# Gate logits of a top-2 mixture of experts from split fp32r operands in one column group, where four column groups multiplied fp32

## The reference

```python
x = L0_attn_data                                   # (4, 512, 1024)
block_mask = mask.reshape(32, 32, 32, 32).sum(axis=(1, 3)) > 0
w_masked = weight * repeat(block_mask)             # (1024, 1024)
x = x + einsum('bsk,nk->bsn', layernorm(x), w_masked)

z = layernorm(x)
logits = z @ W_gate + b_gate                       # 8 experts
_, top_idx = top_k(logits, 2)
y_all = relu(einsum('bsd,edh->bseh', z, W_e) + b_e)
x = x + take_along_axis(y_all, top_idx).mean(over the two)
```

## Time and profile before

| | us |
|---|---|
| median of 3 runs | 709.16 |
| lowest and highest run | 708.97, 710.17 |
| profiled execution | 709.16 |
| its span in the trace | 707.4 |
| TensorE busy | 681.8 |
| VectorE busy | 325.2 |
| ScalarE busy | 240.1 |
| GpSimd busy | 286.6 |

### The profile page before, as it was taken

How to read it: one execution, slowest core, us unless ns; L and a number is a source line. 1 busy time by engine, 2 the same in 40 slices (tenths; PEclk the granted TensorE clock), 3 DMA queues, 4 the chain that set the end, 5 groups by cost and what they waited for, 6 DMA issues and landing times.

```text
span 707.4 us, 11264 instructions
## 1 busy us (share of the span) xinstructions
PE 681.8 (96%) x3617; PEld 559.9 (79%) x3617; DVE 325.2 (46%) x667; ACT 240.1 (34%) x323; POOL 286.6 (41%) x254
## 2 busy tenths in 40 slices
PE   5999999999899999999999999999999999999993
PEld 5667888877678888888888888888888888888883
DVE  4669787888998653343341540351542530000000
ACT  4832212212421434434343434343434343434330
POOL 6421212115445245454445454445454544444330
PEclk9799999999999999999999999999999999999998
DMA  8725445467754459687686683686594855232323
GB/s 318 307 89 176 184 149 209 133 251 249 243 197 150 149 156 245 165 224 202 149 261 151 167 233 82 149 264 150 169 246 101 230 145 115 37 57 34 57 34 56
DMA packets 34501, 118.21 MB, mean 167 GB/s; under 512 B 5776, under 2 KB 5776, under 8 KB 34448
## 3 DMA queue, kind: packets, MB, share of 16 engines
q1 hardware_dynamic: 22032, 80.23, 31.7%
q0 software_dynamic: 11232, 37.23, 25.8%
q10 hardware_dynamic: 1184, 0.04, 0.1%
HBM read 83.40 MB, written 37.75 MB: 171 GB/s over the span
## 4 chain that ended last, share of the span: by engine, by line
PE 85%; DVE 7%; issue 3%; DMA 2%; POOL 1%; SPq 1%; ACT 1%; POOLq 0%; DVEq 0%
PE psO L335 77%; PE psT L437 5%; DMA mask_stage<-L_attn_mask 2%; PE psT L358 1%; DVE st L691 1%; PE psG L470 1%; DVE xr L718 1%; DVE st L699 1%; POOL rs L1035 0%; DVE x2T L718 0%; ACT wT L566 0%; PE psT L376 0%; SPq L273 0%; SPq L274 0%; POOLq L46 0%
## 5 line engine op out<-in xcount | busy, mean ns | idle before, releaser
L335 PE MATMUL psO<-slots,xT 128*128 (+1 forms) x1872 | 435.9, 392 | 0.0
L335 PEld LDWEIGHTS psO<-slots,xT 128*128 128x128 f32 x1872 | 348.2, 188 | 70.7
L335 PE MATMUL psO<-wT,xT 128*128 128x512 f32 x768 | 182.8, 394 | 0.2 <-ACT wT L566 0.2
L335 PEld LDWEIGHTS psO<-wT,xT 128*128 128x128 f32 x768 | 141.7, 188 | 28.6 <-ACT wT L566 0.3
L1081 POOL DMA_INDIRECT rows_out<-xb,tok_of x37 | 63.8, 1725 | 220.9 <-ACT xb L659 214.5
L845 DVE CAST slots<-raw 128x1024 fp32r<-128x1024 f32 x56 | 53.6, 957 | 193.7 <-PE psO L335 105.3
L659 ACT ACTIVATE xb<-psO 128x512 f32<-128x512 f32 x78 | 46.8, 600 | 252.8 <-PE psO L335 252.8
L1075 POOL TENSOR_TENSOR xT<-x2T,xT 128x1024 fp32r<-128x1024 f32 x38 | 100.3, 2640 | 17.7 <-ACT x2T L638 17.4
L847 DVE TENSOR_TENSOR slots<-raw,slots 128x1024 fp32r<-128x1024 f32 x56 | 75.1, 1342 | 1.9
L600 ACT ACTIVATE psO<-bias_slot 128x512 f32 (+1 forms) x78 | 47.1, 604 | 36.7 <-ACT xb L659 17.0
L1020 POOL TENSOR_SCALAR rs<-mv 128x1 f32<-128x1 f32 x16 | 4.5, 280 | 109.1 <-DVE mv L693 109.1
(11 more groups left out here) (162 smaller groups left out, 425.5 us busy)
## 6 DMA issues: line engine op xcount, KB each, us to landing
raw<-L_ffn_W_e SPq DMA_DIRECT2D x56, 512.0 KB, 5.2
xb<-data_t SPq DMA_DIRECT2D x16, 512.0 KB, 4.2
x_rows<-x SPq DMA_DIRECT2D x16, 512.0 KB, 5.1
xr<-L_attn_data SPq DMA_DIRECT2D x11, 512.0 KB, 6.0
rows_out<-xr SPq DMA_DIRECT2D x11, 512.0 KB, 2.7
mask_stage<-L_attn_mask SPq DMA_DIRECT2D x8, 512.0 KB, 11.2
w_stage<-L_attn_weight SPq DMA_DIRECT2D x8, 512.0 KB, 11.8
bias_slot<-L_ffn_b_e SPq DMA_DIRECT2D x8, 512.0 KB, 6.0
```

The costliest lines, as they stand in the source:

```text
L335: last = eng.matmul(psum, xT[:, p, a, kt, :], moving(b, kt), start=(i == 0 and kt == 0 and not seeded), stop=(i == len(PASSES) - 1 and kt ...
```

## The change

The gate product is made from the split operands. `gates` becomes fp32r, with 32 columns for each group of features: HI and LO of each of its two old parts. The 16 matmuls of a block multiply it with `xT`, first its HI and then its LO part, and all accumulate in partitions 0 to 31 of `psG`, that is in one column group. `gated` and `fold` have 32 rows, and L455 adds up the four combinations of HI and LO instead of the four quarters. VectorE makes the LO parts of `gates` once, with two subtractions behind the copies, and the memset of the 16 empty columns goes. As the gate no longer reads `xb`, `load_x` no longer waits for `c_gate`, and it is called for block i + 3 in place of i + 2.

```diff
-        gates = sb("gates", [P, KT, 32], F32)
-        fold = sb("fold", [P, 2 * N_EXP], F32)
-        gated = sb("gated", [P, P], F32)
+        gates = sb("gates", [P, KT, 2, 2, N_EXP], F32R)
+        fold = sb("fold", [4 * N_EXP, 2 * N_EXP], F32)
+        gated = sb("gated", [4 * N_EXP, P], F32)
...
                 if t >= 2:
                     eng.wait_ge(c_xlo, t - 1)
-                    eng.wait_ge(c_gate, t - 1)
...
-                if 2 <= i + 2 < NB:
-                    load_x(i + 2)
+                if 2 <= i + 3 < NB:
+                    load_x(i + 3)
...
-                        eng.wait_ge(c_gw, GATES)
+                        eng.wait_ge(c_gw, 5)
...
-                    for kt in range(KT):
-                        q = kt % N_QUART
-                        last = eng.matmul(psG[32 * q:32 * q + 32, 0:P], gates[:, kt, :], xb[:, i % 2, kt * P:(kt + 1) * P],
-                                          start=(kt < N_QUART), stop=(kt >= KT - N_QUART))
+                    for part in (HI, LO):
+                        for kt in range(KT):
+                            last = eng.matmul(psG[0:4 * N_EXP, 0:P], gates[:, kt, :, :, :].rearrange("p a b e -> p (a b e)"),
+                                              xT[:, i % 2, part, kt, :], start=(part == HI and kt == 0),
+                                              stop=(part == LO and kt == KT - 1))
...
-                    eng.activation(gated[:], psG[:, 0:P], ACT.Copy).then_inc(c_gated, 1)
+                    eng.activation(gated[:], psG[0:4 * N_EXP, 0:P], ACT.Copy).then_inc(c_gated, 1)
...
-            quarters = ident[:].rearrange("p (q x) -> p x q", q=N_QUART)
-            eng.tensor_reduce(fold[:], quarters[:, 0:2 * N_EXP, :], AX.X, ALU.add).then_inc(c_prep, 1)
-            eng.memset(gates[:, :, 2 * N_EXP:], 0.0).then_inc(c_gw, 1)
+            eng.tensor_tensor(fold[:], ident[0:4 * N_EXP, 0:2 * N_EXP], ident[0:4 * N_EXP, 2 * N_EXP:4 * N_EXP], ALU.add).then_inc(c_prep, 1)
...
-            eng.tensor_copy(gates[:, :, 0:N_EXP], wg[:]).then_inc(c_gw, 1)
-            eng.tensor_copy(gates[:, :, N_EXP:2 * N_EXP].rearrange("p (q c) e -> p q c e", q=N_QUART), folded).then_inc(c_gw, 1)
+            of_folded = lambda part: gates[:, :, part, 1, :].rearrange("p (q c) e -> p q c e", q=N_QUART)
+            eng.tensor_copy(gates[:, :, HI, 0, :], wg[:]).then_inc(c_gw, 1)
+            eng.tensor_copy(of_folded(HI), folded).then_inc(c_gw, 1)
             eng.tensor_copy(wg_sum[:], psW).then_inc(c_gw, 1)
+            eng.wait_ge(c_gw, 2)
+            eng.tensor_tensor(gates[:, :, LO, 0, :], wg[:], gates[:, :, HI, 0, :].bitcast(F32), ALU.subtract).then_inc(c_gw, 1)
+            eng.tensor_tensor(of_folded(LO), folded, of_folded(HI).bitcast(F32), ALU.subtract).then_inc(c_gw, 1)
```

More of the change, by code:

```diff
@@ L236, in build @@
         c_first, c_pick = sem("c_first"), sem("c_pick")
-        ST, TOP, HOT, RS1, RS2, GATES = 3, 12, 8, 2, 4, 4
+        ST, TOP, HOT, RS1, RS2 = 3, 12, 8, 2, 4
         FIRST_KNOWN, FIRST_TOK = 4, 15
```

## The result

The changed kernel takes 714.55 us (median of 6 runs, 714.40 to 714.75), the kernel before, on the same chip, 709.07 (6 runs, 708.20 to 710.17). The ratio is 1.0078, with a 95% interval of 1.0065 to 1.0091: slower by 5.5 us. The forecast of 717.3 was right in sign and 2.8 us too high.

A forecast was written before the change was run, and what follows sets the result against it. TensorE was taken to bound most rounds, VectorE six. Gate +0.53 and fold +0.29 us over 16 blocks make 13.1; less 4.8 hidden and 0.2 at the start, +8.1 on 709.2 gives 717.3 us, range 712.8 to 730.

The forecast's parts named there:

- The bound and the place: Token-block loop, 46.6 to 236 us: time added to TensorE is kernel time, except where TensorE waits anyway.
- The step of the narrow fp32r matmul: Gate matmuls in one column group: 0.063 us from start to start, 0.95 from first to last.
- (a): Gate: the next weight load doesn't hide, step 0.083 us, gate +0.83 a block, 722 us; chance 0.12.
- (b): Gate: a narrow fp32r matmul takes 0.11 us like fp32, gate +1.28 a block, 729.5 us; chance 0.10.
- (c): Gate: a narrow fp32r matmul takes 0.229 us like a wide one, gate +3.17 a block, 760 us; chance 0.12.
- The gate's price: Gate matmuls L470 on TensorE: +0.53 us a block, 0.43 to 0.61 by the two readings.
- Rival (d): Gate: matmuls of one column group overlap, step below 0.027 us, drain and fold save up to 0.2 a block, 707; chance 0.03.
- The fold: Fold matmul L455 in a 32-row tile: draining and unhidden weight loads add 0.29 us a block, between 0 and 0.35.
- the case without the fold's cost: Fold matmul's smaller tile needs no drain: ten blocks pay 0.53 us each, 714 us; chance 0.13.
- Six rounds hidden: Six VectorE-bound rounds of the loop hide 4.8 us of their 4.9 us added TensorE time.
- The rest at nothing: VectorE's two subtractions, the dropped memset, ACT's smaller copy and the earlier loads of x: no gain or cost.
- The sum: Whole kernel: 13.1 us for 16 blocks, less 4.8 hidden and 0.2 at the first fold, gives +8.1 us.

The follow-up runs named there:

- the run in one column group: The kernel before with its eight fp32 gate matmuls all in column group 0: 723.80 us, ratio 1.0212.
- the run with 128 rows: The changed kernel, but `gated` and `fold` keep 128 rows, 96 of them zero: 711.58 us, ratio 1.0048.
- the runs in fp32r: The changed kernel with `gated` and `fold` in fp32r instead of fp32: 712.90 us with 32 rows, 710.24 us with 128 rows.
- the changed kernel with spread slices: The changed kernel with the first expert's weight chunks split over rounds 10 to 15 as 1, 1, 2, 1, 2, 1: 713.44 us, ratio 1.0073.

## Why the prediction was right, and where it was off

**The bound and the place: right.** Time added to TensorE in the loop is time of the kernel; nothing changed after 236 us.

**The step of the narrow fp32r matmul: right.** Forecast 0.063 us and 0.95 from first to last; measured 0.0605 and 0.91 (1.13 - 0.22). Rivals (a), (b) and (c), with 0.083, 0.11 and 0.229, are out; the loads of 32 columns add nothing that shows. The 0.11 of a fp32 matmul, which the prediction read from two L420 that are transposes in the code, was borne out by the run in one column group (1.66/15). The Trainium skill's 81 ns a matmul ("TensorE: Matmul & The Clock Gate", "Back-to-back issue gap"), with which the 722 us of (a) agreed, is too high for this stream.

**The gate's price: mis-sized.** This is the term that was off. "First to last start is then 15 x 0.063 = 0.95, against 0.37" counts only what lies inside the group, plus 0.05 for a shorter last stream. But the old group had 0.10 + 0.21 us at its two seams and the new one has 0.03 + 0.06, which is 0.22 saved and not 0.05. So the gate costs 0.54 - 0.22 = +0.32 a block and not +0.53, which lies below the stated 0.43 to 0.61. One seam stood in the rows: the earlier trace rows puts the first L470 0.10 behind the last L376 (65.70 against 65.41 + 0.36 - 0.17 = 65.60), four times the step of that group. Rival (d) did name the drain that would be saved, but as part of a case with a chance of 0.03. The same drain stood in the fold's term, which took it from L391, a fp32 matmul in a narrow tile, and was not carried over to the gate, where it was about to go.

**The fold: right.** Forecast +0.29 a block and 0.66 against 0.37 in the step; measured 0.64 against 0.37, and 0.31 a round with the late start of the projection behind it. The time alone would not have told: 714.55 is nearer to the 714 of the case without the fold's cost. The step of 0.64 and the run with 128 rows show that it was paid, while the gate cost less. The analogy from a change of columns to one of rows held in size; the runs in fp32r show that it is not one thing, since only that of the rows is paid in both types. The Trainium skill, "TensorEngine Tiling (Array Packing)", Key Properties, says that changing the tiling mode drains TensorE. The fold's rows agree (0.26 to 0.27 us in either type), the fp32 gate's too (0.3 for both sides); the fp32r gate's matmuls, in the same 128x32 tile between full ones, show no drain.

**Six rounds hidden: right.** 3.8 us of waits gone, with 0.64 a round, where 0.82 a round was to take all 4.8; doubling the gate in these rounds cost nothing and in others its full price.

**The rest at nothing: right** within half a microsecond, by the run with the loads undone for the loads; the first gate matmul, at 45.5 to 45.8 in the kernels with the new preparation and no long low-clock stretch, is 0.1 to 0.2 later than in those with the old one. VectorE's spare time has grown. Its wait for the projection in one early round, before and after:

```profile
72.09 0.75 DVE L718 SCALAR_TENSOR_TENSOR xr<-psO,kept,xr 128x512 f32<-128x512 f32 x1 [0.38 <-PE psO L335]
72.79 0.75 DVE L718 SCALAR_TENSOR_TENSOR xr<-psO,kept,xr 128x512 f32<-128x512 f32 x1 [1.33 <-PE psO L334]
```

**The sum.** 0.64 in place of 0.82 turns the 8.1 into 16 x 0.64 - 3.8 = 6.4, which is 1.7 of the 2.8 us and fits the 6.1 to 6.2 of executions alike in clock. The other 1.1 is put down to the base: 709.2 had the stretch at 1.2 GHz in it. The page of before shows it as one slice at 0.7 in the row of the granted clock, and the window up to 45 us as a mean of 0.89. A forecast from 708.0 with the gate's seams would have been 714.4.

## What to carry to other kernels

Price a group of matmuls from the last start before it to the first start behind it, before and after, and not from its own first to its own last: its seams can weigh as much as its step. Shrinking an operand to fewer rows saves nothing on TensorE and can cost 0.27 us each time it stands between full tiles; zero rows are cheaper. And before costing added work, find out in which rounds another engine is late: the same 0.44 us cost 0.44 in one round and nothing in another, and a cover that someone later removes turns up as a price (about 8 us in place of 6).

## What the runs showed of the hardware that I had not expected

- A fp32r matmul in a tile of 128 rows and 32 columns, between matmuls of the full array, starts 0.03 us behind them and is followed after 0.06; groups of fp32 ones in such tiles leave about 0.3 for both sides, in the first column group, in the second or spread over four. One matmul in a tile of 32 rows between full ones costs 0.26 to 0.27 us in both types, and its weights are not loaded under the matmul ahead.
- A cast or a tensor_scalar operation of VectorE on eight elements a partition takes 0.17 us, and 0.5 to 3.9 beside a pair of GpSimd's operations of 2.4 us each.
- Behind one wait of TensorE of 3.16 us the matmuls took 1.65 us more, since they ran in part at the lower clock; behind one of 0.55 us (the changed kernel with spread slices) the granted clock stayed at 1.00.
